# Two blocks on one core: when the weight pieces are rounded in the attention stage

## The reference

```
# second block, per sequence
h = film(rmsnorm(x, norm1_w), cond, film1_w, film1_b)
Q, K, V = h @ q_w + q_b, h @ k_w + k_b, h @ v_w + v_b
attn = softmax(Q K^T * 512 ** -0.5)
x = x + (attn V @ proj_w + proj_b)
h = film(rmsnorm(x, norm2_w), cond, film2_w, film2_b)
x = x + gelu(h @ mlp_w1 + mlp_b1) @ mlp_w2 + mlp_b2      # mlp_w1 512x2048, mlp_w2 2048x512
```

## Time and profile before

| what | value |
|---|---|
| median of 3 runs | 1483.64 us (1482.88 to 1484.57) |
| profiled execution, its own time | 1484.56 us |
| its span, first to last instruction | 1482.8 us |
| mean granted clock of TensorE | 1.000 |
| TensorE matmul busy | 1470.2 us (99%), 8712 instructions |
| VectorE busy | 937.5 us (63%) |
| ScalarE busy | 670.1 us (45%) |
| GpSimd busy | 623.4 us (42%) |

### The profile page before, as it was taken

The page is one execution under the profiler, slowest core; times in us unless marked ns, Lnnn a source line. Parts: engine busy times, 40 slices in busy tenths (PEclk is TensorE's granted clock), DMA queues, the critical chain, the costliest instruction groups (busy, mean ns, idle before and its releaser), DMA issues. The chain is left out here.

```text
span 1482.8 us, 24226 instructions
## 1 busy us (share of the span) xinstructions
PE 1470.2 (99%) x8712; PEld 1194.1 (81%) x8712; DVE 937.5 (63%) x1878; ACT 670.1 (45%) x2023; POOL 623.4 (42%) x544
## 2 busy tenths in 40 slices
PE   8999999999999999999999999999999999999999
PEld 5888888888888668878888788888888888888887
DVE  6677777777776676877766644763358434763354
ACT  4656556565553455656766433332324323332210
POOL 5756666666654556766846102401123102401001
PEclk9999999999999999999999999999999999999999
DMA  7222232222213544787554864545464554545332
GB/s 258 69 75 98 72 106 73 79 101 72 81 63 122 194 147 130 252 314 251 202 174 143 305 227 171 170 156 215 162 194 135 195 194 172 169 156 214 135 135 93
DMA packets 92792, 232.58 MB, mean 157 GB/s; under 512 B 9664, under 2 KB 17856, under 8 KB 87552
## 3 DMA queue, kind: packets, MB, share of 16 engines
q1 hardware_dynamic: 90848, 216.24, 42.5%
q10 hardware_dynamic: 1824, 14.79, 2.4%
HBM read 174.17 MB, written 56.82 MB: 156 GB/s over the span
## 5 line engine op out<-in xcount | busy, mean ns | idle before, releaser
L1336 ACT ACTIVATE pa<-bank,neg_max 128x128 f32<-128x128 f32 x512 | 181.8, 409 | 136.4 <-DVE neg_max L1744 136.4
L729 PE MATMUL bank<-w_hi,g_hi 128*128 128x512 f32 x512 | 200.5, 392 | 0.0
L731 PE MATMUL bank<-w_hi,g_lo 128*128 128x512 f32 x512 | 199.3, 389 | 0.0
L730 PE MATMUL bank<-w_lo,g_hi 128*128 128x512 f32 x512 | 199.3, 389 | 0.0
L1227 PE MATMUL bank<-op_hi,ring 128*128 128x512 f32 x448 | 174.9, 390 | 1.3 <-DVE u2p L2170 0.7
L1231 PE MATMUL bank<-op_hi,ring 128*128 128x512 f32 x448 | 174.3, 389 | 0.0
L1229 PE MATMUL bank<-op_lo,ring 128*128 128x512 f32 x448 | 174.3, 389 | 0.0
L2332 POOL TENSOR_TENSOR pa<-pa,rec 128x512 f32<-128x512 f32 x128 | 143.1, 1127 | 54.1 <-DVE rec L1767 53.9
L2304 POOL TENSOR_TENSOR xrc<-xrc,b 128x512 f32<-128x512 f32 x32 | 49.7, 1583 | 267.5 <-DMA xrc<-x_dram 267.5
L1597 ACT ACTIVATE sum<-sum,cols 128x512 f32<-128x512 f32 x128 | 92.0, 722 | 113.6 <-DVE sum L2170 113.5
L1336 ACT ACTIVATION_READ_ACCUMULATOR pa<-bank,neg_max 128x1 f32 x512 | 127.3, 249 | 0.0
(11 more groups left out here) (263 smaller groups left out, 3546.6 us busy)
## 6 DMA issues: line engine op xcount, KB each, us to landing
ring<-w_dram SPq DMA_DIRECT2D x32, 1792.0 KB, 7.5
rows<-st_dram SPq DMA_DIRECT2D x32, 512.0 KB, 4.4
hid_dram<-sum SPq DMA_DIRECT2D x64, 256.0 KB, 2.2
hid<-hid_dram SPq DMA_DIRECT2D x64, 256.0 KB, 2.8
w_dram<-w_parts ACTq DMA_DIRECT2D x8, 1792.0 KB, 7.1
xa<-xt_in SPq DMA_DIRECT2D x32, 256.0 KB, 4.1
xra<-xt_in SPq DMA_DIRECT2D x32, 256.0 KB, 2.8
x_dram<-h SPq DMA_DIRECT2D x32, 256.0 KB, 2.0
```

The lines of the kernel that those rows point to most:

```text
L729: nc.tensor.matmul(dst, w_hi, a_hi, start=start, stop=False)
L730: nc.tensor.matmul(dst, w_hi, a_lo, start=False, stop=False)
L731: return nc.tensor.matmul(dst, w_lo, a_hi, start=False, stop=stop)
L1336: last = nc.scalar.activation(pa[:, j, m, :], scores_bank[j][:, m * P:(m + 1) * P], ACT.Exp, bias=neg_max[:, j * C + m:j * C + m + 1], acc ...
```

## The change

Two things move, and nothing is added or removed in number but one wait.

In the attention stage, in groups 1, 2 and 3 the rounding of the second W1 piece on ScalarE moves from before the first slot to the end of the first slot (b = 0, after `next_h(g, 1)`), and its two low-half instructions on VectorE move from the fourth `h_g` part (m = 3) to the second slot (b = 1, after `copy_ptb`). The groups with one piece are as they were.

In SP's queue the load of the fourth x tile goes ahead of the second residual tile in every group, and the load of W2's second piece is issued behind a wait for the last attend (`bpv` at 32), before the last store of the attention stage; before, it stood behind the landing of all those stores.

```diff
@@ SP, body_b @@
-                for b in range(2):
-                    load_bxr(g, b)
+                load_bxr(g, 0)
                 if not first:
                     load_next(3)
+                load_bxr(g, 1)
                 load_bxr(g, 2)
@@ SP, behind the groups @@
             each_group(body_b)
+            sp.wait_ge(bpv, NB)
+            load_w2(1)
             store_x2(NG - 1, GB - 1)
...
-            sp.wait_ge(bxn, NB + GB)
-            load_w2(1)
@@ ScalarE, body_b @@
                 squares_b(g + 1, 3)
-                for i in w1_pieces(g)[1:]:
-                    split_w1(i)
...
                     if b < GB - 1:
                         next_h(g, b + 1)
+                    if b == 0:
+                        for i in w1_pieces(g)[1:]:
+                            split_w1(i)
@@ VectorE, body_b @@
-                    if m % 2 == 1 and m // 2 < len(w1_pieces(g)):
-                        split_w1(w1_pieces(g)[m // 2])
+                    if m == 1:
+                        for i in w1_pieces(g)[:1]:
+                            split_w1(i)
...
+                    if b == 1:
+                        for i in w1_pieces(g)[1:]:
+                            split_w1(i)
                     if b // 2 < len(w1_pieces(g)):
                         low_sums(w1_pieces(g)[b // 2], b % 2)
```

## The result

The kernel after takes 1495.47 us (median of 4 runs, 1494.42 to 1495.81), the kernel before 1483.29 us beside it (4 runs). The ratio is 1.0078, with a 95% interval of 1.0065 to 1.0090: 12.2 us slower. I had forecast 1482.1 us in a range up to 1485.3. The profiled execution took 1495.17 us with a span of 1493.3.

The account below looks back on a forecast made before the run. PE was taken as the bound, busy 1470.2 of 1482.8 us. Holes closed (-1.92, -0.94) and new waits (+0.4, +0.45, +0.48) gave -1.53 us off 1483.64, so 1482.1 us, range 1480.3 to 1485.3.

Parts of the forecast that it names:

- part 3: SP's queue: fourth tile moved ahead and loads held behind the second W1 load; zero, up to 2.3 us a group.
- rival C: SP's held queue lands x tiles too late, blocking squares, mean square and `tb`: slower, 1486.7 us at its bound; chance 0.05.
- "Zero" for the fourth tile: SP's queue: loading the fourth x tile ahead of a residual load gains nothing, since ScalarE's wait is off PE's path.
- part 1: ScalarE's rounding of the second W1 piece moved behind `next_h(g, 1)`: slot 0 holes in groups 2 and 3 close, -1.92 us.
- Part 2: VectorE's low halves moved to slots 1 and 2: new PE waits at slot 2's attend, 0.88, 0.45, 0.48 us.
- Part 2a: GpSimd overlap with the moved low halves: relief in group 1, its wait 0.4 instead of 0.88 us; groups 2, 3 unchanged.
- Part 4: W2's second piece loaded earlier: the hole before the sixth up product of the second round closes, -0.94 us.

Follow-up runs that it names:

- experiment 3: Kernel before plus SP waits ahead of the second W1 load in groups 1 and 2, no computation moved: 1497.61 us, ratio 1.0090 to the kernel before.
- experiment 4: Kernel before with an added SP wait ahead of the second W1 load in group 1 only: 1488.52 us against 1484.04, ratio 1.0031.
- experiment 6: Kernel after with the second W1 load behind x tiles and query-bias rows, except in group 0: 1484.21 us against 1483.84 for the kernel before, ratio 1.0003.
- experiment 7: Kernel after with group 2's four x_late loads behind the x tiles and query-bias rows: 1495.01 us against 1484.04 for the kernel before, ratio 1.0070.
- experiment 9: Kernel before with only the fourth x tile's load moved ahead of the second residual tile: 1482.19 us, ratio 0.9990.
- experiment 10: Kernel before with SP's two moves and the second W1 piece rounded between the third and fourth x tile's squares: 1480.18 us against 1483.84, ratio 0.9975.

## Why the prediction was wrong

**The step that failed** is in part 3: "I take zero, and up to 2.3 us a group for the range". The mechanism was written down (the second W1 load held for some 8 to 10 us, x tiles behind it, VectorE's mean square and `tb` blocked in order) and was rival C with a chance of 0.05, bounded at 1486.7 us. What was wrong is the size, in two terms. The first is the issue: I had the tiles of group 2 issued at 651.9 us, but the low halves that the W1 load waits for ended at 652.38 (650.83 + 1.55) and not at 649, and the tiles were issued from 655.34. PE was itself 2.0 us behind the kernel before by then (slot 0 at 644.82 against 642.83). The second and larger one is the landing: the second tile needed 10.7 us. I worked with the landings of the earlier trace rows, 2.5 to 7.3 us, as if they were a property of the load, but they came with the traffic of the kernel before. In the kernel after the held queue did not just shift its issues by 10 us: the DMA engines idled (4 GB/s), and then what had been spread came at once (410 GB/s), beside the 1.8 MB stores of ScalarE's queue. The kernel before moved 9.7 MB in the 36 us from 606 to 642, which is 24 us of work at 410 GB/s. A stop of 10 us in them leaves 26 us for 24 us of work, with hardly a reserve. The prediction uses none of the windows' DMA columns. Experiments 3 and 4 show that the hold alone makes such a loss, 6 that the loss goes when the same work is done without it. That the hold acts through the bytes it leaves undone is read from the windows; no run tells it from the later issue alone, and the one expectation that rested on bytes failed (experiment 7).

The Trainium skill ("DMA: Bandwidth & Descriptors", section Rules for kernel authors) says that transfers issued from SP and from ScalarE run on the same 16 DMA engines. The trace agrees: SP's loads landed late beside ScalarE's stores, and the two together stay at 408 to 425 GB/s where the engines are full. The page (section Where 436 GB/s comes from) gives about 435 GB/s for the ports on the SBUF side, and about 358 GB/s per core as what binds transfers between HBM and SBUF, half of what two cores share. This kernel, which runs on one core, was above the second figure with 410 GB/s over 6 us and below the first, and the measurement decides.

**The rest of part 3.** "Zero" for the fourth tile was set for the case that part 1 holds, and no run tests it in that case. By itself the move is worth 1.5 us (experiment 9). And the result stores "have the rest of a group to land" did not hold: one took 16 us, and made group 2's hole and kept the fourth tile back.

**Not foreseen: the clock.** A hole of 5.6 us was followed by 6 us at half clock, 2.9 us more. My price for C had only holes in it.

**Part 1** had the right holes, and where SP is not held they close, in experiment 6 in both groups. That the rounding is their cause is not shown: the fourth tile moved alone takes 1.7 of the 1.92 us (experiment 9), with the rounding where it was. Tile and rounding stood one behind the other, and the prediction put all 1.92 us on the rounding. In the kernel after the hole of group 3 is gone, and in group 2 its place was taken by the late tile (1.7 us).

**Part 2** was right in kind and too small: 0.88, 0.45 and 0.48 us forecast at the attend of slot 2, together 1.81, or 1.33 in the sum; measured 0.78, 0.80 and 0.79, together 2.4, and 0.6 more at the next group's first product, which the sum left out. Mainly for this the forecast gain did not come in experiment 6 either, without the hold (0.85 us at each attend there). **Part 2a**, the relief in group 1, did not come. The two low halves took 1.55 us in each of the three groups instead of the 1.03 of the earlier trace rows; this is group 1:

```profile
615.80 1.55 DVE L1649 TENSOR_TENSOR w_parts<-stage_w,w_parts 128x512 fp32r<-128x512 f32 x2
617.27 1.23 DVE L1649 TENSOR_TENSOR w_parts<-w_sums,w_parts 128x512 fp32r<-128x512 f32 x1
```

GpSimd's additions had moved on as I had expected (they ended at 613.8), and its W1 sums stood in their place, from 613.8 to 618.0: the first piece's load was not late, only the second's was. **Part 4** was right: the hole of 0.94 us is closed in every run with that load moved, though the time alone can't tell 0.9 us.

## What to carry to other kernels

Before an instruction that a DMA queue waits for is moved later, list what is queued behind that wait and count bytes: the transfers of a period over the full rate, against the period less the hold. Such a count warns and does not price: here 24 us of transfers still fitted into 26. Landing times from a trace hold only for the traffic they were taken in. And where an engine waits for a tile between two steps, filler work belongs into that idle time (in experiment 10 the trace shows its gain, the time can't tell it) rather than into a slot in which another engine has 0.15 us to spare.

## What was not expected of the hardware

The result store issued at 621.71 needed 16.0 us to land with the engines full, against at most 7.2 us of the kernel before for this line in that stretch; ScalarE's W1 stores needed 9.3 to 11.2 instead of 7.0 to 7.7. And the granted clock fell to 1.2 GHz in a stage that was busy on either side: after 5.6 us without matmuls the next 6 us had it. The same followed the 4.7 us hole of experiment 7 (512-column matmuls 0.43 us apart for about 5 us, some 2.3 us lost) and the holes of 6.8 and 7.2 us of experiment 3. Why the second hold costs more than the first is partly open: in group 2 the four x_late loads come on top, but moving them back (experiment 7) did not shorten the time; and in experiment 3 the second hold was the longer one, 11.8 us against 8.8.
